# Gathering every row tile of the relation and sum passes by GpSimd's indirect DMA, none row by row from SyncE and ScalarE

## The reference

```
x = x + attention(h, src, dst)                  # softmax of q[src].k[dst] per dst, 4 heads
x = x + relation(h, edge_index, edge_type)      # 8 relations, edges in both directions, mean per relation
x = x + gine(h, edge_attr_16, edge_index)       # sum of h[dst] + edge embedding per src, then an MLP with batch norm
x = x + edge_conv(h, edge_attr_6, edge_index)   # sum of (h W + b)[src] + edge term per dst, ReLU
```

## Time and profile before

| what | value |
|---|---|
| time, median of 3 runs | 21862.58 us (21862.25 to 21864.21) |
| profiled execution, span from its first to its last instruction | 15054.0 us |
| time outside that span, median less span | 6808.6 us |
| POOL busy | 11087.4 us, 74% of the span |
| DVE busy | 9778.7 us, 65% |
| PE busy | 8740.4 us, 58% |
| ACT busy | 2787.6 us, 19% |
| mean granted TensorE clock | 0.656 of full speed |

### The profile page before, as it was taken

How to read it: one execution, slowest core, us unless ns; L and a number is a source line. 1 busy time by engine, 2 the same in 40 slices (tenths; PEclk the granted TensorE clock), 3 DMA queues, 4 the chain that set the end, 5 groups by cost and what they waited for, 6 DMA issues and landing times. The chain is left out here.

```text
span 15054.0 us, 271220 instructions
## 1 busy us (share of the span) xinstructions
PE 8740.4 (58%) x56159; PEld 6734.5 (45%) x56575; DVE 9778.7 (65%) x34050; ACT 2787.6 (19%) x7303; POOL 11087.4 (74%) x11347
## 2 busy tenths in 40 slices
PE   6766667777777777555555555555444444544444
PEld 2212226666666666244444444444333333433334
DVE  8877777777878778866666677777533333433334
ACT  0011114444444444421111111111100000200000
POOL 4777767777777777777777777777677777477776
PEclk8866668999999999865555555555555555655555
DMA  2011122222222222422222222222222222422222
GB/s 85 7 42 50 53 59 74 69 69 69 69 69 69 69 69 67 152 83 59 59 58 59 58 63 63 62 63 63 69 63 63 63 62 60 121 59 59 58 59 68
DMA packets 734382, 992.39 MB, mean 66 GB/s; under 512 B 271737, under 2 KB 534898, under 8 KB 732626
## 3 DMA queue, kind: packets, MB, share of 16 engines
q0 software_dynamic: 387968, 670.55, 17.1%
q1 hardware_dynamic: 324786, 301.13, 6.5%
q10 hardware_dynamic: 20000, 3.33, 0.1%
HBM read 795.25 MB, written 178.86 MB: 65 GB/s over the span
## 5 line engine op out<-in xcount | busy, mean ns | idle before, releaser
L1834 DVE TENSOR_TENSOR acc<-banks,acc 128x128 f32 x3328 | 969.8, 291 | 2616.2 <-PE banks L1792 2247.3
L668 POOL DMA_INDIRECT rec_dst<-stage_dst_sort,row_dst_sort x1563 | 1575.4, 1008 | 641.1 <-issue 474.3
L800 POOL DMA_INDIRECT far_att<-table_qv,recs_att x1664 | 1636.5, 983 | 523.9 <-issue 506.8
L800 POOL DMA_INDIRECT far_sum_dst<-table_h,recs_dst x1613 | 1561.2, 968 | 584.1 <-issue 491.7
L800 POOL DMA_INDIRECT far_sum_src<-table_h,recs_src x1613 | 1572.9, 975 | 558.8 <-issue 491.6
L800 POOL DMA_INDIRECT far_rel_src<-table_xw,recs_rel_src x1638 | 1574.7, 961 | 508.7 <-issue 494.2
L800 POOL DMA_INDIRECT far_rel_dst<-table_xw,recs_rel_dst x1638 | 1561.1, 953 | 510.4 <-issue 494.5
L1622 DVE TENSOR_TENSOR acc<-banks,acc 128x128 f32 x3328 | 969.7, 291 | 1119.2 <-PE banks L1548 1002.5
L936 POOL DMA_INDIRECT rec_src<-moved_att,row_src x1248 | 1245.0, 998 | 397.3 <-issue 379.9
L1792 PE MATMUL banks<-far_sum_src,hot_sum_src 128*128 128x128 f32 x3226 | 825.1, 436 | 1214.9 <-DVE hot_sum_src L1825 831.3
L1792 PE MATMUL banks<-far_sum_dst,hot_sum_dst 128*128 128x128 f32 x3226 | 825.9, 436 | 1147.5 <-DVE hot_sum_dst L1825 899.8
(11 more groups left out here) (343 smaller groups left out, 21302.0 us busy)
## 6 DMA issues: line engine op xcount, KB each, us to landing
lone_sync_rel_dst<-table_xw SPq DMA_DIRECT2D x3328, 0.5 KB
lone_sync_rel_src<-table_xw SPq DMA_DIRECT2D x3328, 0.5 KB
lone_sync_sum_src<-table_h SPq DMA_DIRECT2D x3328, 0.5 KB
lone_sync_sum_dst<-table_h SPq DMA_DIRECT2D x3328, 0.5 KB
lone_scalar_sum_src<-table_h ACTq DMA_DIRECT2D x3200, 0.5 KB
lone_scalar_sum_dst<-table_h ACTq DMA_DIRECT2D x3200, 0.5 KB
table_xw<-xw_rel_tables SPq DMA_DIRECT2D x98, 512.0 KB
far_att<-table_qv,recs_att POOLq DMA_INDIRECT x1664
```

Of the source, the lines that this page charges most:

```text
L668: e.indirect_dma_start(out=flat_dst, out_offset=bass.IndirectOffsetOnAxis(ap=row["dst"][:, c + i:c + i + 1], axis=0), in_=stage["dst"][:, ...
L800: e.indirect_dma_start(out=self.far[:, g % RING, t, :], out_offset=None, in_=table, in_offset=bass.IndirectOffsetOnAxis(ap=index, axis=0)) ...
L1834: e.tensor_tensor(acc[:, bass.ds(at[t], 1), :], sums[g0 % 4][:, t:t + 1, :], acc[:, bass.ds(at[t], 1), :], ALU.add).then_inc(k.s_sum, 1)
```

## The change

All tiles go through `Stream.gather`. The constants `LONE` and `LONES`, the `lone` and `ids` buffers, their semaphores, and the functions `fetcher`, `tiles`, `far_rows`, `fetched`, `turns`, `mine`, `number_rows`, `fetch_rows` and `single_rows` are gone. SyncE is left with the loads of records (and of a few parameters), ScalarE with its copies. The core of the diff:

```diff
     def gather(self, e, g, table, column):
-        for t in self.tiles(g):
+        for t in range(GT):
             index = self.rows(g, column, column + 1)[:, t, :].bitcast(I32)
             e.indirect_dma_start(out=self.far[:, g % RING, t, :], out_offset=None, in_=table,
                                  in_offset=bass.IndirectOffsetOnAxis(ap=index, axis=0)).then_inc(self.k.s_ring[g % RING], 16)

     def gathered(self, g):
-        return self.k.s_ring[g % RING], self.ring_base[g % RING] + 16 * sum(len(self.tiles(h)) for h in range(g % RING, g + 1, RING))
+        return self.k.s_ring[g % RING], self.ring_base[g % RING] + 16 * GT * (g // RING + 1)
...
# relation_pass and sum_pass, sync
                 st.load(e, c)
-                if c:
-                    single_rows(c - 1)
-            single_rows(BLOCKS - 1)
...
# relation_pass and sum_pass, tensor
-                    st.fetched(e, g0)
+                    e.wait_ge(*st.gathered(g0))
...
-                        i = e.matmul(sums[g0 % 3][:, t, :], hot_s[:, g0 % 4, t, :], st.far_rows(g0, t), start=True, stop=True)
+                        i = e.matmul(sums[g0 % 3][:, t, :], hot_s[:, g0 % 4, t, :], st.far[:, g0 % RING, t, :], start=True, stop=True)
...
# sum_pass, scalar
-            numbered = {1: st.number_rows(e, "scalar", 1, IDX)}
             for j, (w0, n) in enumerate(WIN4):
...
-                s = j + 1
-                if s >= LONES:
-                    continue
-                if s >= 3:
-                    e.wait_ge(k.s_product, p0 + (s - 1) * LONE)
-                e.wait_ge(k.s_ids["scalar"], numbered[s])
-                if s + 1 < LONES:
-                    numbered[s + 1] = st.number_rows(e, "scalar", s + 1, IDX)
-                st.fetch_rows(e, "scalar", s, k.table_h, 0, P)
```

More of the change, by code:

```diff
@@ L769, with __init__ @@
 class Stream:
-    def __init__(self, k, s, recs, far=None, lone=None, ids=None):
+    def __init__(self, k, s, recs, far):
         self.k, self.rec, self.recs, self.far = k, k.rec[s], recs, far
-        self.lone, self.ids = lone or {}, ids
-        self.rec_base, self.ring_base, self.lone_base = k.rec_base, list(k.ring_base), {n: list(b) for n, b in k.lone_base.items()}
+        self.rec_base, self.ring_base = k.rec_base, list(k.ring_base)
     def load(self, e, c):
@@ L849, in close @@
         self.k.rec_base += 16 * (BLOCKS // NREC)
[L850 to L854, removed]
+        self.k.ring_base = [self.gathered(GROUPS - RING + r)[1] for r in range(RING)]
 assert BLOCKS % NREC == 0 and GROUPS % RING == 0
@@ L1455, in relation_pass @@
         sb = scratch(k, ctx, f"rel_{side}")
-        lone, ids = {"sync": sb("lone_sync", [P, 2, F])}, {"sync": sb("ids_sync", [1, 2, P], I32)}
-        st = Stream(k, side, sb("recs", [P, NREC, BT, COLS[side]]), sb("far", [P, RING, GT, F]), lone, ids)
+        st = Stream(k, side, sb("recs", [P, NREC, BT, COLS[side]]), sb("far", [P, RING, GT, F]))
         win, acc, more, n_more, n_att = k.win[side], k.acc, k.more[side], MORE[side], ATTRS[side]
@@ L1700, in sum_pass @@
         sb = scratch(k, ctx, f"sum_{side}")
-        lone, ids = {n: sb(f"lone_{n}", [P, 2, F]) for n in ("sync", "scalar")}, {n: sb(f"ids_{n}", [1, 2, P], I32) for n in ("sync", "scalar")}
-        st = Stream(k, side, k.recs[side], sb("far", [P, RING, GT, F]), lone, ids)
+        st = Stream(k, side, k.recs[side], sb("far", [P, RING, GT, F]))
         HOT = 5
@@ L1791, in tensor @@
                 for t in range(GT):
-                    i = e.matmul(sums[g % 4][:, t, :], hot[:, g % HOT, t, :], st.far_rows(g, t), start=True, stop=True)
+                    i = e.matmul(sums[g % 4][:, t, :], hot[:, g % HOT, t, :], st.far[:, g % RING, t, :], start=True, stop=True)
                 i.then_inc(k.s_product, 1)
```

45 lines of the change are left out of this document (1 added, 44 removed).

## The result

The kernel after takes 19499.64 us (median of 4 runs, 19481.15 to 19512.2), the kernel before beside it 21863.4: ratio 0.8915, 95% interval [0.8902, 0.8928]. The forecast was 22058 us, 0.90% more than before; measured were 10.8% less. The sign is wrong, and the time lies outside the range.

What follows compares the result with a forecast made beforehand. POOL's gathers, one every 1.25 us, were taken to bound the four passes. 154 added gathers gave 195.9 us, all other terms 0; added to the 21862.6 us median this made 22058.5 us, +0.90%, range 21940 to 22155.

Steps and rivals of the forecast that it cites:

- What lies outside: Median minus trace span: 6808.6 us taken to lie outside the trace and to stay, so the sum is added to the median.
- Nobody waits for it: Single row DMAs of SyncE and ScalarE in the four passes: POOL never waits on them, so removing them gives 0.
- SyncE's 80%: SyncE's busy share of a pass: 15.93 us on 32 rows of the 20 us a block takes.
- The gathers' term: Relation and sum passes: 154 added POOL gathers, hidden by no work, each at its pass's own step, 195.9 us more.
- the second rival: Gathers in the four passes get quicker once the row DMAs go: 84.1 us more, 21947 us, chance 0.12.
- Stretched: Every POOL step is longer in the timed execution, scaling the added gathers by 1.452 to 284.5 us: 22147 us, chance 0.23.
- The outside part belongs to the instructions or the row DMAs: The 6808.6 us are spent per instruction; dropping 41,888 of 271,220 takes away 1051 us: 21007 us, chance 0.08.
- No change: Added gathers hide because POOL is not the bound in the timed runs: 21863 us, chance 0.07.
- The rule on issuing engines: Skill's rule that several issuing engines save only small sequencer time: undoing the spread costs 0 in place of 195.9 us.

Runs made afterwards that it cites:

- e1: The kernel before, unchanged, run again with a trace of its own: 21889.41 us, ratio 1.0002.
- e2: The kernel after, unchanged, run again: 19478.11 us, ratio 0.8908 to the kernel before.
- e8: Kernel before without ScalarE's rows; GpSimd gathers every tile, SyncE still fetches its single rows, which TensorE no longer uses: 21897.18 us, ratio 0.9833.
- e16: Kernel before without ScalarE's single rows, the sum passes' record loads moved from SyncE to ScalarE; long setting: 22222.18 us, ratio 1.0151.
- e17: Kernel before without SyncE's single rows, ScalarE's kept in the sum passes; long setting: 20866.58 us, ratio 0.9532.
- e11: The kernel after, unchanged, in the short setting: 15222.28 us beside 15029.84 of the kernel before, ratio 1.0123.
- e7: Kernel before without ScalarE's single rows and with SyncE's for every 32nd group in place of every 16th: 20144.58 us, ratio 0.9049.
- sets A, E and F: Sets of runs, each on one chip; the kernel before takes 21873.46 us in A, 15055.46 in E, 21883.05 in F.
- e5: Kernel before with a quarter of the gathers in the relation and sum passes, single rows kept: 17585.28 us, ratio 0.7897.
- e18: The same edit of the kernel before as e5, run in another set, long setting: 17421.88 us, ratio 0.7958.

## Why the prediction was wrong, by its own steps

**The step that failed is "What lies outside".** It took the difference of 6808.6 us between time and span for a lump that a sum made on the span can be added to. In all 19 executions profiled after it time and span differ by 1.7 to 1.8 us. The Trainium skill (Runtime: NRT & Kernel Launch, "The ~15µs preamble/postamble breakdown") gives some 15 us for what surrounds a kernel. The runs show less outside the span and decide, and by either number the gap of 6808.6 us could not lie outside; that the trace was not of an execution like the timed ones would have followed. The prediction noted the factor of 450 and kept the lump. Between the two the attention pass alone differs by 5352 - 3816 = 1536 us, which has no single rows.

**"Nobody waits for it"**, the 0 for the single rows, is the term that turned the sign: together with the added gathers the four passes gave -2354 us between e1 and e2. It holds in the trace that it was read from, though the list of POOL's waits could not show it alone, since it is TensorE that waits for single rows (its list there has no such wait either). It does not hold in the timed runs. SyncE's 80% left 4 us a block, and with the record load, 17.33 us from load to load, less than 3; 32 rows at 27.09 us in place of 15.93 overrun the 23.4 us that a block of the kernel after takes there (2434.8/104), by 5 us with the loads, 104 times a pass: 28.48 x 104 - 2434.8 = 527 us, measured 460.9. e8 is the test of that: with TensorE not waiting for the rows the loss stays, so in this kernel it is the record loads behind them that cost. e16 and e17 bound the reading: with no load behind them, the rows themselves are waited for and cost as much. What costs is an issuing engine that needs longer for its rows than the gathers around them take; who waits for it depends on what stands in its queue.

**The gathers' term** has the right size where its condition holds: 195.9 forecast, 192.4 measured in e11. By pass, from first to last gather, e11 has 2081.5, 2091.3, 2129.1 and 2129.1 us against those of the earlier trace rows: +22.0, +18.1, +65.0 and +76.8, forecast 32.7, 32.9, 65.3 and 64.9. In the relation passes the mean gather got shorter (1575.63/1664 = 947 ns against 953 in the earlier trace rows, and 953 against 961), which is 9.8 and 13 us, about what is missing, a sliver of the second rival; in sum src the mean stayed at 975 ns, and in sum dst it rose from 968 to 975. In the long setting e2's POOL starts a gather every 1.464 us in relation dst, its waits for TensorE included. What 154 gathers more are worth there no run shows.

**The rivals.** *Stretched*: the gathers do not stretch, their median is 944 ns in the profile after. The step from gather to gather did, from 1.258 to 1.769 us in e1's relation dst, by waits that the change takes away, so that no added term scales with it. *The outside part belongs to the instructions or the row DMAs* had the right side, and half of its name: it is the row DMAs, 2354 us net of the added gathers, inside the execution and not outside, and not by number (e7) but because they overrun a block. Its 0.08 was too little, because the argument against it ("a program's instructions already run inside the span") spoke only of the trace at hand. *No change* named the condition that came true, that POOL is not the bound in the timed runs, and priced it on DVE and TensorE alone, not on SyncE.

**The rule on issuing engines.** The short setting speaks as the prediction said: the spread over three engines saves 192 us, POOL's 1.25 us a tile, while the DMA engines are 0.21 to 0.23 busy. In the long one the spread loses 2354. The Trainium skill (DMA: Bandwidth & Descriptors, "Issuing engines are not separate DMA queues") states that such a spread saves the sequencer's time alone, and the traces agree; they do not agree that this time is small, for it is what both settings turn on, once gained and once lost.

**What stays open.** What puts a set into one setting or the other: sets A, E and F bear the same chip number, so the number does not decide it (whether it is the same piece of silicon is not known). And why the row DMAs slow down while gathers run in the long setting; e5, e18 and the two paces within e1 show that they do, no run shows by what.

## What to carry to other kernels

Hold the span of a trace against the timed median before reading anything else. Here they were apart because the trace was of an execution in the other setting, and its slack was not the slack of the timed one; take no sum from such a trace until one matches. An engine that only issues DMAs and has 20% to spare can become the bound: write down what it has per block, and what it would cost at 1.7 times its step, the factor of this case. The choice between these two kernels depends on the setting: the kernel before is 1.2% quicker in the short one, the kernel after by 10.9% in the long one, and no variant here beats both in both.

## What the runs showed of the hardware

One program with one input has two settings, 15.03 to 15.06 ms and 21.86 to 22.27 ms, constant within a set of runs. In the four passes TensorE's granted clock is no cause: it is 0.50 to 0.51 of full speed in e11's and 0.54 to 0.58 in e1's, the higher one in the longer passes, both at or near the lower level of 1.2 GHz. In the attention pass it is 0.92 in the earlier trace rows and 0.76 in the profile after, and what that costs was not taken apart. The gathers themselves are alike (944 to 947 ns), and so are the transfers: the packets of the gathers' queue take the same time in both settings, 17.1% of 15054.0 us and here 11.8% of e1's 21836.7, 2574 and 2577 us.

```profile
q0 software_dynamic: 387968, 670.55, 11.8%
```

What differs is how other engines go on beside them. In the long setting VectorE waits longer for the same thing. First the profile after, then e11:

```profile
DVE over_top_att L1058 <- remote: 2304.5, 408, 6.3
```

```profile
DVE over_top_att L1058 <- PE banks L957: 489.3, 416, 3.3
```

The wait of over_top_att comes once a group in both. It lasts 1.2 us in the short setting and ends 0.04 us after TensorE's last instruction of L957 (median of 416); in the long one it lasts 5.6 us, and 3.63 us lie between that instruction's end and VectorE's start, with nothing in the trace to fill them. TensorE too has stretches in which its instructions come late, here in e2 beside running gathers (sum src):

```profile
16562.64 0.28 PEld L1674 LDWEIGHTS banks<-far_sum_src,hot_sum_src 128*128 128x128 f32 x1 [1.80 <-issue]
...
16564.04 0.37 PE L1674 MATMUL banks<-far_sum_src,hot_sum_src 128*128 128x128 f32 x1 [1.73 <-issue]
...
16566.13 0.37 PE L1674 MATMUL banks<-far_sum_src,hot_sum_src 128*128 128x128 f32 x1 [1.73 <-issue]
```

One matmul in 2.09 us, with nothing that the trace shows to wait for; in e11 eight of them go in 2.05 us:

```profile
11604.48 2.05 PE L1674 MATMUL banks<-far_sum_src,hot_sum_src 128*128 128x128 f32 x8 [2.93 <-DVE hot_sum_src L1707]
```

Most matmuls follow each other as quickly in both; the stretches show in TensorE's waits on this line that end in issue, 1027.6 us in 626 times in e2 and 518.1 us in 157 in e11. So it is not a matter of row DMAs: instructions of SyncE, ScalarE and TensorE come late beside GpSimd's indirect DMAs, in the one setting and not in the other. That the gathers cause it is shown for the rows of SyncE (e5, e18); for TensorE's stretches it is read from one timeline.
